# A mixture-of-experts layer on one core: earlier row tables for the first ten expert tiles, and the shared expert's last two tiles moved to the end

## What is computed

```python
x = L0_attn_x                                    # 8 x 512 tokens, 256 wide
x = x + attn(layernorm(x), Wq, Wk, Wv)           # causal, one head of 256
xn = layernorm(x)
shared = (silu(xn @ shared_gate.T) * (xn @ shared_up.T)) @ shared_down.T
probs = sigmoid(xn @ router_w.T + routing_bias)  # 8 experts
scores, indices = top_k(probs, 2); scores = scores / sum(scores)
g = silu(einsum('th,ehi->tei', xn, gate_w)); u = einsum('th,ehi->tei', xn, up_w)
out = x + shared + einsum('tei,eih,te->th', g * u, down_w, w)   # w: scores of the two chosen experts
```

## Time and profile before

| what | us |
|---|---|
| median of 3 runs | 559.57 (558.17 to 560.89) |
| span of the profiled execution, first to last instruction | 555.3 |
| TensorE busy in it | 518.0 |
| last matmul ends at | 545.0 |
| mean granted TensorE clock | 0.986 of full |

### The profile page before, as it was taken

The page is one execution under the profiler, slowest core; times in us unless marked ns, Lnnn a source line. Parts: engine busy times, 40 slices in busy tenths (PEclk is TensorE's granted clock), DMA queues, the critical chain, the costliest instruction groups (busy, mean ns, idle before and its releaser), DMA issues.

```text
span 555.3 us, 14903 instructions
## 1 busy us (share of the span) xinstructions
PE 518.0 (93%) x4757; PEld 425.5 (77%) x4757; DVE 369.8 (67%) x980; ACT 301.0 (54%) x580; POOL 288.9 (52%) x242
## 2 busy tenths in 40 slices
PE   4889988999999999997999999999999999999992
PEld 3557766788878888886767788888787888888881
DVE  5788998689887878899747555445454454454551
ACT  3989877678777676744233443433343433434341
POOL 4466677668676765857022344452444434434443
PEclk9999999899999999998899999999999999999998
DMA  8799848949694947414465965764846536345443
GB/s 271 201 181 208 178 127 158 217 133 209 161 208 141 194 127 170 155 70 136 131 115 85 98 107 69 103 83 60 108 59 89 73 60 97 55 65 78 62 58 38
DMA packets 139351, 68.55 MB, mean 123 GB/s; under 512 B 114608, under 2 KB 132336, under 8 KB 139280
## 3 DMA queue, kind: packets, MB, share of 16 engines
q1 hardware_dynamic: 126128, 48.84, 43.5%
q0 software_dynamic: 13152, 18.76, 19.4%
HBM read 19.46 MB, written 23.08 MB: 77 GB/s over the span
## 4 chain that ended last, share of the span: by engine, by line
PE 65%; DVE 12%; DMA 8%; SPq 5%; ACT 5%; issue 3%; POOL 1%; POOLq 0%; ACTq 0%; DVEq 0%
PE bank L2216 29%; PE bank L2240 15%; PE bank L2547 4%; PE bank L2322 3%; PE bank L2564 3%; DMA v<-xnrow 2%; PE bank L2625 2%; PE bank L2347 2%; PE bank L2392 2%; DMA xn2t<-xrow 2%; PE bank L2369 2%; PE bank L2640 2%; SPq L405 2%; DMA x<-x 1%; DVE h L1470 1%
## 5 line engine op out<-in xcount | busy, mean ns | idle before, releaser
L2216 PE MATMUL bank<-xn2t,w 128*128 128x256 f16 x1608 | 184.9, 273 | 1.3 <-DVE th L1653 1.1
L2216 PEld LDWEIGHTS bank<-xn2t,w 128*128 (+1 forms) x1608 | 155.2, 98 | 24.3 <-DVE th L1653 2.2
L1644 DVE SCALAR_TENSOR_TENSOR th<-th,bank 128x512 f32<-128x512 f32 x83 | 56.6, 682 | 55.2 <-ACT th L989 54.1
L2240 PE MATMUL bank<-w,h 128*128 (+1 forms) x768 | 91.5, 273 | 0.0
L943 ACT ACTIVATE h<-th 128x512 f16<-128x512 f32 (+1 forms) x69 | 42.9, 622 | 84.6 <-DVE th L1653 78.3
L989 ACT ACTIVATE th<-bank 128x512 f32<-128x512 f32 x83 | 49.2, 593 | 62.1 <-PE bank L2216 47.6
L2240 PEld LDWEIGHTS bank<-w,h 128*128 128x128 f16 x768 | 74.0, 98 | 10.4 <-DVE x L1676 0.3
L866 POOL DMA_INDIRECT out<-p,wm x28 | 43.9, 1569 | 67.2 <-ACT p L1323 27.3
L1470 DVE TENSOR_TENSOR h<-th,h 128x512 f16<-128x512 f32 (+1 forms) x69 | 50.6, 733 | 38.3 <-ACT h L943 38.1
L734 POOL TENSOR_TENSOR w<-wst,w 128x768 f16<-128x768 f32 x36 | 59.1, 1645 | 18.9 <-ACT w L943 18.7
L758 POOL DMA_INDIRECT rows<-xrow,sidx x56 | 56.5, 1009 | 17.0 <-issue 13.3
(11 more groups left out here) (188 smaller groups left out, 808.4 us busy)
## 6 DMA issues: line engine op xcount, KB each, us to landing
wst<-w_all SPq DMA_DIRECT2D x36, 384.0 KB
x<-x SPq DMA_DIRECT2D x8, 512.0 KB, 5.6
out<-x SPq DMA_DIRECT2D x8, 512.0 KB, 4.0
rows<-xrow POOLq DMA_DIRECT2D x1, 1192.5 KB, 6.6
rows<-xrow,sidx POOLq DMA_INDIRECT x56
out<-p,wm POOLq DMA_INDIRECT x28
xn2t<-rows SPq DMA_TRANSPOSE x26
wm<-rows SPq DMA_DIRECT2D x26, 9.0 KB, 2.4
```

The source lines that it names most:

```text
L1644: d.scalar_tensor_tensor(out=tb, in0=tb, scalar=1.0, in1=G[half][:, :], op0=ALU.add, op1=ALU.mult).then_inc(f_sg, 1)
L2216: ins = mm(dst, w_ap(j, ws, m * MAT + k * I + (2 * half + i) * P, P), moving(ms * KD + k), start=(cnt == 0), stop=(cnt == 3 * KD - 1))
L2240: ins = mm(o[:, a * D:(a + 1) * D], hb[:, (hs * KI + i) * TT + a * P:(hs * KI + i) * TT + (a + 1) * P], w_ap(j, ws, 2 * MAT + i * D, D), s ...
```

## The change

- **Tables in two rounds.** `counts_seen` takes the counts after batch 5 (`SEEN` = 6 batches). From them `table_of_quads` places 5 blocks of 512 rows, which hold routed rows of the first six batches only: pair tiles 0 to 9. Blocks are now cut forwards from a region's start. The other tables (16 more pair tiles, singles, halves) come from the full counts, all under `tab2`: 26, 16 and 14 steps, with half tiles of DVE's other work between them.
- **Order.** `AHEAD` = 14 shared tiles stand before the routed rows. Then come four plain pair tiles (`plain_groups`), between which batch 7 is normalised, transposed and routed, then `first_groups` with the first singles, and the groups as before.
- **Padding.** `zero_rows` fills only the spare region. `zero_ends` (SP) copies 128 padding rows behind each of the eight regions' ends, from DRAM to DRAM, at row numbers read from `end_tab`, after `tab2`; `rows_complete` waits for these and for the scatters of batches 6 and 7.
- **Weight chunks** 29 to 35: on ACT `w_scale` and `w_high` of a chunk stand together and ahead of the tiles' work; on SP chunks 34 and 35 are loaded behind the first pair tile's rows; on POOL `w_low` comes ahead of batch 6's scatters.
- **The end.** The last two shared tiles run after the last pair tile (the last hidden tile into `h_last` = `v`). SP waits for all adds, reads the two tiles' rows of `out` back into `x1`, DVE adds the down products, SP stores them (256 rows, then 128 and 128).
- `half_down` loads 128 columns of `h_h` instead of 64.

```diff
+SEEN = 6
+QUADS = -(-(SEEN * S * TOPK - E * (2 * TT - 1)) // (2 * TT))
+EARLY = 2 * QUADS
+MORE = PAIRS - EARLY
+LATE = 2
+AHEAD = SHARED - LATE
+PLAIN = 2
...
 # SP
             w_load(31)
             w_load(32)
+            out_base(4)
             w_load(33)
-            out_base(4)
-            w_load(34)
-            w_load(35)
...
+            def zero_ends():
+                for e in range(E):
+                    end = sp.value_load(end_tab[0:1, e:e + 1], min_val=0, max_val=ROWS - P)
+                    sp.dma_start(rows[ds(end, P), :], rows[SPARE:SPARE + P, :]).then_inc(pads_in, 16)
+            def rows_complete():
+                sp.wait_ge(rows_in[0], scattered(B - 2))
+                sp.wait_ge(rows_in[1], scattered(B - 1))
+                sp.wait_ge(pads_in, 16 * E)
...
             sp.wait_ge(tab, T_STEPS)
             pair0, pair1 = pair_row(0), pair_row(1)
             sp.wait_ge(rows_zero, 16)
-            sp.wait_ge(rows_in[0], scattered(B - 2))
-            sp.wait_ge(rows_in[1], scattered(B - 1))
-            load_pair_rows(pair0, 0, 2 * SHARED - 4)
-            load_pair_rows(pair1, 1, 2 * SHARED - 4)
+            sp.wait_ge(rows_in[0], scattered(SEEN - 2))
+            sp.wait_ge(rows_in[1], scattered(SEEN - 1))
+            load_pair_rows(pair0, 0, 2 * AHEAD - 2)
+            w_load(34)
+            w_load(35)
+            load_pair_rows(pair1, 1, 2 * AHEAD)
             load_pair_aux(pair0, 0, 0, 0)
+            load_pair_aux(pair1, 1, 0, 0)
+            out_base(5)
+            out_base(7)
+            out_base(6)
+            pair_rows(2)
+            pair_aux(2)
+            pair_rows(3)
+            pair_aux(3)
+            pair_rows(4)
             sp.wait_ge(tab2, T2_STEPS)
+            zero_ends()
+            rows_complete()
+            single_rows(0)
+            single_rows(1)
+            pair_rows(5)
+            pair_aux(4)
+            single_aux(0)
             first_groups()
...
+            for i in range(LATE):
+                sp.dma_start(tile_of(AHEAD + i), tile_rows(AHEAD + i)).then_inc(back_in[i], 16)
+            sp.wait_ge(y_read, AHEAD + PAIRS + 1)
+            sp.dma_start(tile_rows(AHEAD), tile_of(AHEAD)).then_inc(out_done, 16)
+            for a in range(2):
+                n = 2 * (SHARED - 1) + a
+                sp.wait_ge(z_put, a + 1)
+                sp.dma_start(out[n * P:(n + 1) * P, :], x1[:, n * D:(n + 1) * D]).then_inc(out_done, 16)
+            sp.wait_ge(out_done, 16 * (B + 3))
...
 # DVE, behind places(6), row_numbers(6), the lows of tile 11, gate and up of tile 12
+            add_shared(10)
+            table_of_quads()
+            ffn_low(12, 0)
+            ffn_gate(13, 0)
+            ffn_low(12, 1)
+            add_shared(11)
+            ffn_up(13, 0)
...
+            def plain_groups():
...
+                route(7)
+                ffn(t + 2, 0)
+                weights(7)
+                places(7)
+                row_numbers(7)
+                ffn(t + 2, 1)
+                k = table_of_pairs()
+                ffn(t + 3, 0)
+                k = table_of_singles(k)
+                ffn(t + 3, 1)
+                table_of_halves(k)
...
 # PE, behind shared_gate_up(12, 0) and (12, 1)
             shared_down(10, 1, 2)
             shared_gate_up(13, 0)
-            last_transposes(0)
-            last_transposes(1)
+            shared_down(11, 0, 2)
             shared_gate_up(13, 1)
...
             shared_down(12, 0, 2)
-            shared_gate_up(15, 0)
-            shared_down(13, 0, 2)
-            shared_gate_up(15, 1)
-            shared_down(14, 0, 2)
...
+            def plain_groups():
+                pair_gate_up(0, 0)
+                shared_down(13, 0, 2)
+                pair_gate_up(0, 1)
+                last_transposes(0)
+                last_transposes(1)
+                pair_gate_up(1, 0)
+                pair_down(0)
+                pair_gate_up(1, 1)
+                logits(7)
+                pair_gate_up(2, 0)
+                pair_down(1)
+                pair_gate_up(2, 1)
+                prefix(7)
+                pair_gate_up(3, 0)
+                pair_down(2)
+                counts()
+                pair_gate_up(3, 1)
             def first_groups():
...
+                pair_gate_up(p, 0)
+                pair_down(p - 1)
+                pair_gate_up(p, 1)
                 pe.wait_ge(tab2, T2_STEPS)
                 single_gate_up(0, 0, 16)
...
             def last_group():
...
+                gate_up(t, 0, 0, half_batch(xn24(B - 1), 0), True)
+                pair_down(PAIRS - 1)
+                gate_up(t, 1, 0, half_batch(xn24(B - 1), 0), True)
+                gate_up(t + 1, 0, 0, half_batch(xn24(B - 1), 1), True)
+                gate_up(t + 1, 1, 0, half_batch(xn24(B - 1), 1), True)
+                down(t, 0)
+                last_down()
```

More of the change, by code:

```diff
@@ L74, in partners @@
 def partners(n):
-    return n % 2 == 0 and (n < EARLY or n == PAIRS - 2) and ADDED["pair", n + 1] == ADDED["pair", n] + 32
-def place(n):
-    return n + 2 if EARLY <= n < PAIRS - 2 else n - MORE if PAIRS - 2 <= n < PAIRS else n
+    return n % 2 == 0 and n < EARLY and ADDED["pair", n + 1] == ADDED["pair", n] + 32
 def after(kind, n):
@@ L992, in split_h @@
             def split_h(t, half):
-                shared = isinstance(t, int) and t < SHARED
+                shared = isinstance(t, int) and t < AHEAD
                 if shared and t < 0:
@@ L999, in split_h @@
                     act.wait_ge(dump_in, 16)
-                wait(act, dn_mm, t * 2 - (4 if shared else 2) + half + 1)
-                copy((h_of_tile(t) if shared else h)[:, half * 512:(half + 1) * 512],
+                if not (isinstance(t, int) and t == AHEAD + PAIRS + 1):
+                    wait(act, dn_mm, t * 2 - (4 if isinstance(t, int) and t <= AHEAD else 2) + half + 1)
+                copy(h_of_tile(t)[:, half * 512:(half + 1) * 512],
                      th[:, half * 512:(half + 1) * 512]).then_inc(f_hi, 1)
@@ L1402, in y_copy_of, with y_copy_of_single @@
                 y_copy(n, n % 4, 16 * (n // 4) + 16, after("pair", n - 4))
+            def y_copy_of_single(k):
+                y_copy_single(k, k if k < 4 else k % 2, 16 if k < 4 else 16 * (k // 2),
+                              after("single", k - 4 if k < 6 else k - 2))
+            def plain_groups():
+                t = AHEAD
+                tanh(t, 0)
+                xn2_normalise(7, 0)
+                split_h(t, 0)
+                xn2_high(7, 0)
+                xn2_normalise(7, 1)
+                tanh(t, 1)
+                xn2_high(7, 1)
+                split_h(t, 1)
+                tanh(t + 1, 0)
+                last_xn2_t_high(1)
+                last_xn2_t_high(0)
+                split_h(t + 1, 0)
+                act.wait_ge(tab, T_STEPS)
+                expert(0)
+                y_copy_of(0)
+                tanh(t + 1, 1)
+                logits_exp(7)
+                split_h(t + 1, 1)
+                for n in range(2, 2 * PLAIN):
+                    ffn_half_and(t + n, 0, n - 1)
+                    y_copy_of(n - 1)
+                    ffn_half(t + n, 1)
@@ L1801, in table_of_quads @@
-                c.then(d.scalar_tensor_tensor(out=BASE, in0=CNT, scalar=-float(TT), in1=base[0:1, 0:E],
-                                              op0=ALU.add, op1=ALU.add)); c.last()
+                c.then(d.tensor_scalar(ti[0:1, 4 * E:5 * E], CNT[0], 0.0, None, ALU.add)); c.last()
+                units(c, 0, 2 * TT); c.last()
+                c.then(d.tensor_copy(EIGHTS, ti[0:1, 0:E])); c.last()
                 sums_before(c, EIGHTS, INC, PREV)
-                table(c, QUADS, 2, 0, 2 * TT, INC, PREV, BASE)
+                table(c, QUADS, 2, 0, 2 * TT, INC, PREV, base[0:1, 0:E])
@@ L2174, in _ @@
+            plain_groups()
+            first_groups()
+            with dve.Fori(PLAIN + 2, SINGLES - 4 + PLAIN) as i:
                 group(i)
[L2175 to L2176 removed]
+            group(SINGLES - 4 + PLAIN, single=False)
+            for i in range(SINGLES - 3 + PLAIN, GROUPS):
                 group(i, single=False, half=False)
[L2178 to L2180 removed]
```

758 lines of the change are left out of this document (347 added, 411 removed).

## The result

The changed kernel takes 581.48 us (median of 4 runs, 578.98 to 584.98), beside 559.05 for the kernel before (558.17 to 560.89): 1.040 of it, 95% interval 1.035 to 1.045. Beside the second group of experiments it was run again: 580.25 beside 557.20, 1.042 (1.036 to 1.048). The forecast was 590 (572 to 601), slower with a chance of 0.90.

What follows compares the result with a forecast made beforehand. TensorE, busy 93% of the span, bounds the kernel; its matmul sum stays, so only idle stretches count. 555.3 + 12.3 + 21.7 + 5.4 − 6.2 − 2.9 = 585.6 us of span, plus 4.3: 590 (572 to 601).

Steps and rivals of the forecast that it cites:

- First wait of part 1: Before the first pair tile: TensorE at shared_down(11) waits 3.2 us, behind chunk 33's two ScalarE passes, tanh and VectorE's add.
- part 1: The stretch before the first pair tile: two new TensorE waits, 3.2 and 9.1 us, together 12.3 us lost.
- Second wait: TensorE at shared_down(12) waits 9.1 us, as chunk 34 is issued only behind the first table and pair tile 0's load.
- What I left out of the sum: At low(12,1), GpSimd's pass on chunk 34 ends 0.4 us later; by the lock-out rule up to 1.6 us more.
- Part 2: Plain pair tiles and tables: VectorE about 1 us short at tile 2, waits 3.35, 3.05, 14.25 before single tile 0: 21.7.
- Clock: Half speed behind the waits of 9.1 and 14.25 us costs 2 × 2.7 = 5.4 us.
- The end: Last matmul to end of span takes 7.4 us against 10.3: a gain of 2.9 us (1.9 to 5).
- the read-back covered: At the end, copy, two adds, landing and read-back take 11 us, hidden by 2 us under five half products (13.5 us).
- the transition: The 3.1 us wait at the last shared down product, 2.7 at half speed, 0.4 before the first single tile: 6.2 gained.
- the step from span to time: The median of the runs, 559.57, is 4.3 us over the profiled span, so 585.6 becomes 589.9, said as 590.
- A: Rival, faster: chunk 34 and the pads are early enough, so the waits aren't there: 551 us. Chance 0.07.
- B: Rival: one of the two large waits (chunk 34 or the pads) isn't there: 578 or 573 us. Chance 0.15.

Runs made afterwards that it cites:

- second group: Four kernels on one chip beside the kernel before (557.20 us): changed kernel again 580.25, without reads back 580.50, more work ahead of single tile 0 558.63, two queues 557.52.
- The last experiment: Changed kernel with chunks and padding early, pair tile 5's first half moved up, three padding copies on ScalarE, batch 6's row numbers later: 557.52 us, 1.000 of the kernel before.
- the first experiment: Changed kernel with weight chunks 34 and 35 issued behind chunk 33, ahead of SyncE's wait for the first table: 579.10 us, 1.032 of the kernel before.
- the fourth experiment: Changed kernel with eight more register reads and copies of the same size behind the eight padding copies, into rows nothing reads: 592.24 us in one run.
- the last two versions: Changed kernel with chunks and padding early and pair tile 5's first half ahead of single tile 0, 558.63 us; same with three copies on ScalarE and row numbers later, 557.52.
- the first group: Four variants of the changed kernel beside the kernel before (561.17 us): chunk 34 early 579.10, padding early 576.94, both 570.00, eight copies more 592.24.
- the kernel with pair tile 5 first: Changed kernel with chunks and padding early, pair tile 5's first half and pair tile 4's down product ahead of single tile 0: 558.63 us, 1.003 of the kernel before.

## Why the prediction came out as it did

Direction and mechanism held: the two large waits, their lengths, their causes and the order of events are as forecast. The size is too large: the terms add up to 30.3 us of loss, the medians differ by 22.4, and the time is 8.5 us under the number given.

**First wait of part 1: 3.2 forecast, 2.0 found** (1.72 ahead of shared gate/up 13, 0.3 ahead of down product 11). Its step was ScalarE's two passes on chunk 33. In fact chunk 33 was at work from 230.1 as forecast, but tanh(12,0) had been held by VectorE's row numbers of batch 6 and a landing of scattered rows behind them. TensorE therefore stood one product earlier, and this wait covered part of the other. The last experiment bears the cause out.

**Second wait: 9.1 forecast, 9.0 found** and 8.9 in the second execution, each of its stations within 0.3 us: the load at 238.7 (238.9), chunk 34 at 240.06 (240.2), its pass at 244.18 (244.4), the down product at 248.87 (248.8). The length is what was forecast; that the clock times agree as well is chance, since tile 12 began 1.2 us later than in the kernel before and the first wait was 1.2 us shorter. What I left out of the sum, VectorE held by GpSimd's pass, showed as 1.15 us for the low half instead of 0.7. Not foreseen was the second chain beneath it, which the first experiment laid open.

**Part 2: 0.6, 3.48, then 1.61, then 14.44 us; forecast 1 (0 to 2), 3.35, 3.05, 14.25.** The third is no miss: the gate/up product between the two took 4.15 us at the lower clock instead of 2.78, and 1.61 + 1.37 is 3.0. The last table ended 15.5 us behind counts() (15.4). The copies took 1.23 us each (1.16), a copy 2.6 us from issue to landing by the page's median (3.0), and the fourth experiment shows that the issue and not the landing is what they cost.

**Clock: 5.4 forecast, 4.9 found** (2.5 and 2.2 us over full speed in the two products, 0.2 in the one behind the first); in the second execution 3.3.

**The end: gain of 2.9 forecast, 4.9 found, and the step to it was wrong in two places.** I had VectorE's add, issue, a landing of 3.0 and 3.65 us more behind the last matmul (which add up to 7.55, not 7.4). The last stores' issue ended at 577.9 and the span 2.0 us later, so what followed the last landing in the kernel before does not come on top of the stores' own landing (2.1 us in this trace). What it was there is open. On the other side I had the read-back covered with 2 us to spare: ScalarE's copy, two adds, a landing. This took GpSimd as free, which it isn't: pair 24's adds started at 560.66, 6 us after ScalarE's copy, behind the landing of pair 23's, and pair 25's at 567.24 behind those. The earlier trace rows showed this wait (2.45 us for `out<-p,wm`), and I read it as a price of the end and not as a queue. The first error made the forecast of the end too long, the second too short.

**The sum.** 555.3 + 11.0 + 20.1 + 1.4 + 0.4 (ahead of the first single down product) + 4.9 − 6.2 − 4.9 = 582.0, against 585.6 in the forecast and 579.9 in the trace.

- 3.6 of the 8.5 us are the terms above: the first wait, the small ones of part 2, the end.
- 2.1 are in no term. The kernel before had small waits of 3.1 us beyond the transition (2.6 for `v<-xnrow`, 0.5 at the end), of which 1.1 are left; that makes 2.4 with the 0.4 counted above. Tile 12's later start takes 1.2 of it back. The remaining 0.9 is open.
- 2.6 are from the step from span to time. 581.59 is 1.7 over its span, as the executions of the kernel before beside the experiments are 1.7 to 1.9 over theirs. The 4.3 that I had added held 1.7 of this kind; for the rest, the profiled execution of the kernel before was about 2 us faster than its median, and that of the changed kernel was not.

The prediction's own bounds, 579 to 598, count the 1.5 us of a landing once below and twice above.

**Rivals.** A (neither wait there) and B (one of them not there) were refuted for this kernel. With the edits something like them comes: with the chunk and the copies early the loss falls from 22 to 9 us, and with 5.2 us more of work ahead of single tile 0 to within the measurement. But A's 551 isn't reached. In the last two versions part 1 keeps 4.4 and 4.7 us of waits and part 2 4.9 and 3.6, most of them for VectorE, and the row of adds holds the end.

## What to carry to other kernels

Of a step that is moved, write down what stands behind it in each queue: both large waits were one instruction (a chunk's load, eight copies) behind a wait that it did not need. A wait found in the profile may have a second one just beneath it; here 2.2 of the 9 us stayed when its first cause was gone. And when the pace of one engine is made shorter, look for a serial chain elsewhere for whose end nobody has waited yet, here adds that each wait for the landing of those before.

## What the runs showed of the hardware

The loss after an idle time of TensorE did not follow its length. These are the times of the 24 matmuls behind a wait (behind the longest, a single tile's 12), against 2.78 us at full speed (2.76), without those in the slow stretches told below:

| idle, us | the product behind it, us |
|---|---|
| 1.6 to 1.9 (seven executions) | 2.79 each |
| 2.2 | 4.45, 4.35, 4.45, but 2.78 in the kernel with pair tile 5 first |
| 2.4, 2.5 | 4.46, 2.79 |
| 3.1 (kernel before) | 5.30 |
| 3.5, four executions at one place | 2.79, 2.79 (after 3.8), 4.15, 5.30 |
| 7.5 | 4.39 |
| 8.9 to 9.1 | 4.34, 5.28, 4.12, 4.92 |
| 11.8 to 23.8 | 4.53 to 4.98 in five executions |

The granted clock was 0.50 behind one of the waits of 3.5 us (292.9 to 298.2, without the reads back) and 1.00 behind another (289.6 to 292.3, the changed kernel again), with the same order of instructions up to there. So the waits of 2.2 to 3.8 us here cost 0 to 2.5 us in the product behind them, the longer ones 1.3 to 2.5, and one of 2.2 us could cost as much as one of 9.

In the four kernels of the first group TensorE, ScalarE, VectorE or SyncE crawled or stood still for 2 to 5 us somewhere between counts() and single tile 0, each with its inputs there (5.29 us on ScalarE with chunk 34 early, 3.43 on VectorE ahead of the tables with the padding early). In the second group, and in the changed kernel's first execution, it was in none. It took 3 to 5 us of the gain of the first three. It does not come from the edits alone, since the kernel with pair tile 5 first has both of them and not the stretch. Whether it belongs to that chip or to the profile is open.
